# Attention of a decoder layer: TensorE's order written by two steps, with one value product cut in two blocks of 256 columns

## The reference

```python
q = (x @ wq.T + bq) @ vq.T + vbq      # k and v in the same way
scores = einsum('cbqh,cbkh->cbqk', q, k) / sqrt(16)
attn = softmax(scores, axis=-1)
o = einsum('cbqk,cbkh->cbqh', attn, v)
```

## Time and profile before

| what | value |
|---|---|
| median of 3 runs | 2124.9 us (2123.53 to 2125.03) |
| span of the profiled execution | 2122.5 us |
| PE busy, share of the span | 97% |
| DVE, ACT, POOL busy | 78%, 62%, 23% |
| mean granted TensorE clock | 0.989 |
| attention | from 343 to about 1692 us |

### The profile page before, as it was taken

How to read it: one execution, slowest core, us unless ns; L and a number is a source line. 1 busy time by engine, 2 the same in 40 slices (tenths; PEclk the granted TensorE clock), 3 DMA queues, 4 the chain that set the end, 5 groups by cost and what they waited for, 6 DMA issues and landing times.

```text
span 2122.5 us, 39702 instructions
## 1 busy us (share of the span) xinstructions
PE 2067.2 (97%) x11249; PEld 1165.3 (55%) x11264; DVE 1659.3 (78%) x1727; ACT 1314.4 (62%) x2429; POOL 491.5 (23%) x878
## 2 busy tenths in 40 slices
PE   9999999999999999999999999999999999988996
PEld 4788775444444444444444444444444387767874
DVE  4333356888899999999999998999898576886687
ACT  0112113778888888888888888888888742454344
POOL 0000001121212221221122122212121371465245
PEclk9999998999999999999999999999999999999997
DMA  4456735555575665664665646655647578773672
GB/s 164 139 159 155 186 112 109 84 123 137 100 139 120 108 136 97 131 143 95 135 128 101 141 103 123 137 99 126 138 99 179 182 267 306 278 254 124 222 262 101
DMA packets 214414, 315.25 MB, mean 149 GB/s; under 512 B 105424, under 2 KB 121808, under 8 KB 202064
## 3 DMA queue, kind: packets, MB, share of 16 engines
q1 hardware_dynamic: 214352, 314.47, 58.9%
HBM read 211.06 MB, written 101.19 MB: 147 GB/s over the span
## 4 chain that ended last, share of the span: by engine, by line
PE 86%; DVE 6%; ACT 2%; SPq 2%; DMA 2%; issue 1%; POOL 1%; DVEq 0%; POOLq 0%; ACTq 0%
PE psum L542 26%; PE psum L551 23%; PE psum L187 22%; PE psum L223 11%; PE psum L88 2%; DVE stats L1392 1%; ACT probs L616 1%; DVE y L1517 1%; PE psum L1312 1%; DVE gates L1491 1%; DVE gates L1488 1%; SPq L208 1%; ACT gates L1241 1%; DVE y L1422 0%; DMA x_block<-in_x_t_dram 0%
## 5 line engine op out<-in xcount | busy, mean ns | idle before, releaser
L230 DVE TENSOR_REDUCE neg_max<-psum 128x1 f32<-128x1024 f32 x1024 | 1206.0, 1220 | 135.2 <-PE psum L223 135.0
L616 ACT ACTIVATE probs<-psum 128x512 f32<-128x512 f32 x2048 | 1065.3, 606 | 273.5 <-PE psum L542 269.3
L542 PE MATMUL psum<-q_op,k_op 50*128 50x512 f32 x2048 | 750.3, 449 | 3.9 <-ACT probs L616 1.4
L542 PEld LDWEIGHTS psum<-q_op,k_op 50*128 50x128 f32 x2048 | 353.6, 191 | 580.2 <-ACT probs L616 565.3
L223 PE MATMUL psum<-k_op,q_op 48*128 48x512 f32 x2048 | 620.2, 479 | 1.0 <-DVE neg_max L230 1.0
L551 PE MATMUL psum<-probs,v_op 128*32 128x512 f32 x4096 | 548.1, 607 | 5.8 <-ACT probs L616 2.9
L223 PEld LDWEIGHTS psum<-k_op,q_op 48*128 48x128 f32 x2048 | 389.0, 315 | 21.1 <-issue 4.4
L187 PE MATMUL psum<-x_wino,conv_w 128*128 128x512 f32 x1152 | 276.0, 395 | 1.0 <-DMA conv_w<-conv_w_parts_dram 1.0
L187 PEld LDWEIGHTS psum<-x_wino,conv_w 128*128 128x128 f32 x1152 | 214.4, 188 | 47.0 <-issue 1.3
L241 POOL CAST neg_max_parts<-neg_max 128x8 fp32r<-128x8 f32 x128 | 24.5, 191 | 887.8 <-DVE neg_max L230 887.8
L551 PEld LDWEIGHTS psum<-probs,v_op 128*32 128x32 f32 x4096 | 82.5, 108 | 136.8 <-ACT probs L616 70.0
(11 more groups left out here) (103 smaller groups left out, 1629.8 us busy)
## 6 DMA issues: line engine op xcount, KB each, us to landing
q_op<-qk_parts_dram SPq DMA_DIRECT2D x384, 128.0 KB, 4.1
conv_w<-conv_w_parts_dram SPq DMA_DIRECT2D x32, 1536.0 KB, 6.9
qk_parts_dram<-qk_parts SPq DMA_DIRECT2D x128, 256.0 KB, 3.2
k_op<-qk_parts_dram SPq DMA_DIRECT2D x384, 64.0 KB, 4.0
conv_w_parts_dram<-conv_w_parts SPq DMA_DIRECT2D x16, 1536.0 KB, 6.1
attended_dram<-out SPq DMA_DIRECT2D x64, 256.0 KB, 2.2
attended_parts_dram<-o_parts SPq DMA_DIRECT2D x128, 128.0 KB, 2.5
gates<-in_ctx_dram SPq DMA_DIRECT2D x32, 512.0 KB, 7.7
```

The costliest lines, as they stand in the source:

```text
L230: nc.vector.tensor_reduce(ops["max"][b][:, t:t + 1], mem["pair"][t % 2][:], AX_X, ALU.max, negate=True).then_inc(ops["maxed"], 1)
L542: nc.tensor.matmul(score_bank(i, n, j, last), kop[i][r, j // 2, n // 2 * P:(n // 2 + 1) * P], qop[i][r, j // 2, j % 2 * HALF:(j % 2 + 1) * ...
L616: nc.scalar.activation(probs[n % DEEP][:, j, :], score_bank(k, n, j, last), ACT.Exp, scale=SCALE).then_inc(exp_done, 1)
```

## The change

TensorE's order is written for two steps at a time (n even, tiles t to t + 7, units u to u + 3). V is a value product, a half of it is its four matmuls over 256 of the 512 columns:

- tile t, tile t+1, unit u, tile t+2, first half of V of step n-1
- unit u+1, tile t+3, tile t+4, second half of V of step n-1
- unit u+2, tiles t+5, t+6, t+7, unit u+3, then V of step n, its two halves one behind the other.

Before, two steps had the pattern (four tiles, two units, V) twice. The number of score matmuls is the same. Each value product has 16 matmuls and 16 weight loads in the trace's counting instead of 8 and 8, each matmul over 256 columns. In odd steps the tiles are taken in the order 1, 0, 3, 2, so that tile t uses lane t % 2, and ACT follows that order. A unit's lane 0 always comes first. The ring, the buffers, the other engines' instructions and all DMAs are as before; the copy of bank 7 on ACT stands, as before, behind the first exponential of step 1.

```diff
-            def pv(s, k, n):
-
-                pe.wait_ge(exp_done, s * (STEPS * TILES) + n * TILES + TILES + RING)
+            def values(s, k, n, half):
+
+                if n == 0 and half == 0:
+                    pe.wait_ge(v_ready, s + 1)
+                    pe.wait_ge(pv_out, s + 1)
+                if half == 0:
+                    pe.wait_ge(exp_done, s * (STEPS * TILES) + n * TILES + TILES + RING)
+                cols = slice(half * (HALF // 2), (half + 1) * (HALF // 2))
                 for j in range(TILES):
                     kt = n // 2 + QT // 2 * ((n + j) % 2)
-                    mm = nc.tensor.matmul(pv_bank[32 * j:32 * j + 32, :], vop[k % 2][:, j // 2 * QT + kt, :],
-                                          probs[n % DEEP][:, j, :], start=(n == 0), stop=(n == STEPS - 1))
-                mm.then_inc(pv_step, 1)
+                    mm = nc.tensor.matmul(pv_bank[32 * j:32 * j + 32, cols], vop[k % 2][:, j // 2 * QT + kt, :],
+                                          probs[n % DEEP][:, j, cols], start=(n == 0 and half == 0),
+                                          stop=(n == STEPS - 1), skip_group_check=True)
+                if half == 1:
+                    mm.then_inc(pv_step, 1)
...
+                for n in range(0, STEPS, 2):
+                    t, u = n * TILES, 2 * n
+                    shifted(it, k, t, last)
+                    shifted(it, k, t + 1, last)
+                    unit(it, k, u, 0, last)
+                    shifted(it, k, t + 2, last)
+                    values_before(n, 0)
+                    unit(it, k, u + 1, 0, last)
+                    shifted(it, k, t + 3, last)
+                    shifted(it, k, t + 4, last)
+                    values_before(n, 1)
+                    unit(it, k, u + 2, 0, last)
+                    shifted(it, k, t + 5, last)
+                    shifted(it, k, t + 6, last)
+                    shifted(it, k, t + 7, last)
+                    unit(it, k, u + 3, 0, last)
+                    values(s, k, n, 0)
+                    values(s, k, n, 1)
```

More of the change, by code:

```diff
@@ L529, in _, with shifted @@
             pe.wait_ge(v_out, 4 + PROJECTED // 3)
[L531 to L534, removed]
+            def shifted(it, k, t, last):
+                n, c = t // TILES, t % TILES
+                j = c ^ n % 2
+                r = slice(LANE * (t % 2), LANE * (t % 2) + ROWS_SHIFT)
+                cell = k * (STEPS * TILES) + t
+                wide = cell - WIDE_FROM * TILES
+                if n == 0 and c % 2 == 0:
+                    pe.wait_ge(max_in[k][j // 2], (it + 1) * MAXES + DMA)
                 if last and RING <= wide < 2 * RING:
@@ L544, in s2, with unit @@
+                nc.tensor.matmul(score_bank(k, t, last), kop[k][r, j // 2, n // 2 * P:(n // 2 + 1) * P],
+                                 qop[k][r, j // 2, j % 2 * HALF:(j % 2 + 1) * HALF],
                                  start=True, stop=True).then_inc(s2_full, 1)
-            def pv(s, k, n):
-                pe.wait_ge(exp_done, s * (STEPS * TILES) + n * TILES + TILES + RING)
+            def unit(it, k, u, lane, last):
+                s = it * 4 + k
+                ahead = k + 1 if u < QT else k + 2
+                if last and ahead >= 4:
+                    return
+                if u == QT:
+                    pe.wait_ge(op_in[ahead % 4], (it + ahead // 4 + 1) * OPS)
+                pe.wait_ge(maxed, s * 16 + u + LEAD - 1)
+                b, t = 1 - u // QT, u % QT
+                score_lane(nc, mem, ops, ahead % 4, b, t, lane)
+                score_lane(nc, mem, ops, ahead % 4, b, t, 1 - lane).then_inc(s1_full, 1)
@@ L591, in _ @@
                 slot(LAST, k, last=True)
-            pv(LAST * 4 + 3, 3, STEPS - 1)
+            for half in range(2):
+                values(LAST * 4 + 3, 3, STEPS - 1, half)
         @block.scalar
```

27 lines of the change are left out of this document (14 added, 13 removed).

## The result

The change makes the kernel slower, by 4.4% and more: its four runs took 2207.5, 2227.5, 2264.8 and 2320.3 us (median 2246.1) against 2124.6 us (median of four) before. The ratio of 1.0436 [1.0386, 1.0487] is that of the two faster runs, since the two slow ones are over 1.5% above the fastest and are left out of it. Forecast were 2116. The profiled execution is the one of 2264.8; its span is 2263.0 us, 140.5 more than before.

What follows compares the result with a forecast made beforehand. PE was taken to be bound by a loop of tile 0, exponential 0, tile 3, value product. Two steps at 5.22 us saved 6.7 in the loop and 3.3 in written-out slots, less 1 at the start: 2116 us, range 2098 to 2131.

Steps and rivals of the forecast that it cites:

- A: PE's scores tile, tile, unit, tile ahead of the first half value product of two steps: 0.92 us.
- half: Half value product on PE, two passes fewer, standing between scores: 0.57 us.
- B: PE's scores unit, tile, tile between the two separate half value products: 0.81 us.
- V: Value product at the end of two steps, two halves back to back on PE: 1.00 us, as a whole one.
- C: PE's scores unit, three tiles, unit ahead of the last value product: 1.28 us without a wait, 1.35 with it.
- The wait at t+7: Load of tile t+7 waits for tile t+4's exponential on ACT, 0.66 us into C; costs 0.07 in two steps.
- rival 1: The wait at t+7 does not bind: two steps take 5.15 us, 17 us more won, 2099; chance 0.13.
- rival 2: Joints on PE all slightly dearer: 15 us, 2120 to 2131; chance 0.19 shared with rival 5, plus 0.05 for its slower rest.
- Rival 3: Value passes of 256 columns don't hide their weight loads: 37 us, 2153, slower; chance 0.12.
- Rival 4: Time at tile 3 can't be won, PE spends it emptying the array: 35 us, 2160, slower; chance 0.06.
- Other engines: Term for DVE, ACT, POOL, SP: no new waits, no DMA moves; ACT copy's 0.09 us a slot goes.
- rival 5: One more half-clock stretch of four slow steps costs 4 to 6 us: 2121; chance 0.19 shared with rival 2.

Runs made afterwards that it cites:

- SP edit: Last stores of maxima moved ahead of SP's wait and reading back; kernel before with it 2116.1 us, changed kernel with it 2106.9 us.
- after_flat_sp: Changed kernel with TensorE's loop written out and SP's last stores of maxima moved earlier: 2107.9 us, ratio 0.9927 to the kernel before.
- before_flat_sp: Kernel before with TensorE's loop written out and SP's last stores of maxima moved earlier: 2118.7 us, ratio 0.9971.
- after_sp: Changed kernel, loop and halves kept, with only SP's last stores of maxima moved earlier: 2106.9 us, ratio 0.9919 to the kernel before.
- before_sp: Kernel before with only SP's last stores of maxima moved earlier: 2116.1 us, ratio 0.9961.
- after_sp_pause: after_sp with a wait for a later slot's operands added on TensorE, 15 times: 2382.8 us (2311 to 2397).
- before_sp_pause: before_sp with the same wait for a later slot's operands added on TensorE, 15 times: 2187.0 us, ratio 1.031.
- part 3: Changed kernel with SP's stores moved, 2106.9 us; variants of the new order with slots 0 and 1 in the old order, 2100.0 and 2099.8 us.
- before_halves: Kernel before, old order and loop kept, every value product cut into two back-to-back halves of 256 columns: 2219.4 us, ratio 1.0435.
- halves_sp: before_halves with SP's last stores of maxima moved earlier: 2219.2 us, ratio 1.0452 to the kernel before.
- after_fill: Changed kernel with the pair's last value product over 512 columns and 256 bare semaphore increments added to TensorE's loop body: 2390.8 us (2334 to 2470).
- fill_sp: after_fill with SP's last stores of maxima moved earlier: 2326.1 us, ratio 1.0951 to the kernel before.
- after_flat: Changed kernel with TensorE's hardware loop over slots 4 to 59 written out, so no branch: 2297.9 us, ratio 1.0817 to the kernel before.
- before_flat: Kernel before with TensorE's hardware loop over slots 4 to 59 written out: 2148.9 us, ratio 1.0122.

## Why the prediction was wrong

**What held.** A 0.91, half 0.57, B 0.79, V 1.00, C 1.34, and 5.18 us for a pair. The wait at t+7 is where it was put (its load comes 0.67 us into C, at 600.93 in the kernel after; 0.66 was forecast), so rival 1 is refuted; the joints are not dearer, as rival 2 had it. The back-to-back halves cost 5.24 - 5.23 = 0.01 a pair in the old order; its bound was 0.06 a product. Rival 3 would have shown a half product above 0.57, rival 4 a pair above 5.35. (Rival 4 was also summed too low: by its own words the units' loads, two of 0.15, are lost beside the third crossing, which makes 0.44 x 247 = 109 us and not 35.) The loop with the SP edit takes 83.07 us for four slots against 84.0, 13 us over 14 passes, where 6.7 was the estimate for the loop. The Trainium skill, "TensorE: Matmul & The Clock Gate", section "The mechanism", has a weight load overlap a matmul in flight only where it is for other rows. The trace disagrees for passes of 256 columns too: 16 value matmuls and their 16 loads, all for the same 128 rows, take 1.00 us, as 8 and 8 of 512 columns did. The Trainium skill, "TensorEngine Tiling (Array Packing)", section "Key Properties", has a change of the tiling mode drain TensorE. The trace doesn't show a drain by itself; three crossings in two steps cost what rows of before said.

With the store moved, the order is worth what was forecast for it: after_flat_sp is 10.8 us below before_flat_sp, after_sp 9.2 below before_sp, by the medians, and the forecast was 9. That they agree is in part luck, since the loop gives 13 instead of 6.7 and the start takes up to 26 instead of 1.

**The step that failed** is in "Other engines": "POOL's copy of the values and SP's loads wait for counts that are reached within a microsecond of where they were, with many us to spare. No DMA moves". I had looked at the counts that SP's waits need, and not at the queue behind such a wait. The store of the maxima stands there behind the landing of another DMA, and its own landing was what released the tile that needs it, in 16 of 28 slots of before. So the path had a second releaser with a slack of nothing, where the prediction has "many us to spare". Whatever makes the store late by some tenths now stops PE: a slot is shorter by 0.2 us, the result's store took up to 4.5 us to be read back (3.3 at most before), and instruction packets hold SP up. Moving this one store takes the changed kernel from 2207 to 2320 us down to 2101 to 2129, so without that wait the loss is not there; the tile then has 1.3 us to spare and more. The trace of before showed it, in the 6.3 and 6.1 pairs and the record of 0.46 us.

**The second** is rival 5's size. It priced a stretch at half clock at 4 to 6 us, from the single case at the start, which was the old order's. In the new order 38 pairs ran at half clock and cost 132 us over the full pace, of the 170.5 in the table; the estimate above, over all stretches, is 126. That a stretch lasts longer in the new order is measured (after_sp_pause against before_sp_pause, and the starts in part 3); why it lasts longer was not found, only that the passes of 256 columns are not it. The first steps, charged with 1 us, ran up to 64.9 us at half clock; a pair loses 3.49 in its 8.67 there, which makes 26.

**The third** was no term at all: the length of the program. I counted passes and columns, not that each fp32 matmul is four PE instructions. The loop went from 1233 to 1765. Here the traces show that bodies of 1233 and 1509 never miss, and that 1745 (before_halves, halves_sp) and 1765 (after_fill, fill_sp) miss at 9 to 10 of 13 branches, with PE idle for 6.4 to 9.7 us each time. The Trainium skill, "Runtime: NRT & Kernel Launch", "Instruction fetch mechanics", says that TensorE holds 128 KiB or 2048 instructions in blocks of 16 KiB, and that a taken branch whose target is not in the window of two blocks waits for a DMA. The trace agrees on the block (q8 packets of 16 KB) and on the stall. It doesn't agree on the window: with two blocks held every branch back would have missed in before too, and none did. It was a rival that should have had a chance.

**What stays open.** The changed kernel's loop misses at 5 of 13 branches, and with SP's store moved at none, though PE's program is the same; the other two long bodies, 1745 and 1765, miss with and without it. So length can't be the whole rule, and timing has a part in it. Where a body lies among the 16-KB blocks could tell one body from another, but not after from after_sp; no run varied it. Each count of misses is that of one traced execution, though the ten runs of after_sp, none above 2129 us, leave little room for misses in any of them. Nor is it known why the landing of the result's store took 3.4 to 4.5 us in some slots. The shares of the two causes in the loss can't be added up: without the branch the kernel was slower still (after_flat, where instruction packets flow all along and single issues on SP take up to 1.9 us), without the late store there was no miss. That a miss brings late stores is seen in the fourth slots; how a late store brings a miss is not known.

## What to carry to other kernels

When an order gets shorter by tenths, read each queue behind its waits: for every DMA that the path needs, when it was issued, what stood ahead of it, when it landed, and when it was due; a zero there is a rival with a price. Price a pause of TensorE as its length plus the half-clock stretch that such a pause has been seen to bring in that very order. Before cutting a matmul in two inside a hardware loop, count the body's instructions, and look in the trace for instruction packets between the branches.

## What the runs showed of the hardware

- In the new order a pause of PE of 1.8 to 4.6 us was followed by 78 to 85 us at 1.2 GHz with PE busy all the time, in other cases by 7 to 10; in the old order pauses of 1.2 to 4.9 us were followed by 3.4 to 10.2 where the clock fell at all.
- A branch back that misses leaves PE idle for 6.4 to 9.7 us (4.2 and 4.4 in two cases), and the pass behind it fetches the body again, a 16-KB packet every 10 to 20 us. after_flat has 32 packets more than before_flat for 8192 more PE instructions, 64 bytes each.
- DMA issues on SP are longer beside instruction packets. Of the loads of L206 and L208 between 345 and 1600 us of the kernel after, 12 of the 48 within 0.5 us of such a packet took over 1.1 us, of the other 610 four did. SP's timeline beside the branch above, where the same forms take 0.42 and 0.65 us just before:

```profile
702.39 0.42 SPq L206 DMA_DIRECT2D q_op<-qk_parts_dram  x1
703.02 0.65 SPq L208 DMA_DIRECT2D k_op<-qk_parts_dram  x1
...
704.38 1.26 SPq L208 DMA_DIRECT2D k_op<-qk_parts_dram  x1
705.73 1.61 SPq L206 DMA_DIRECT2D q_op<-qk_parts_dram  x1
```
